# The attention mixer of a small transformer tower, rewritten for fp32 heads in strips of TensorE

## The reference, cut to what matters

```python
E, H, D = 192, 12, 16
h = _ln(x, ln1_g, ln1_b)                     # x is _layernorm(h), a second norm follows at once
qkv = h @ in_w.T + in_b
q, k, v = (t.reshape(B, N, H, D) for t in jnp.split(qkv, 3, axis=-1))
scores = jnp.einsum('bqhd,bkhd->bhqk', q, k) / jnp.sqrt(jnp.float32(D))
attn = jax.nn.softmax(scores, axis=-1)
ctx = jnp.einsum('bhqk,bkhd->bqhd', attn, v).reshape(B, N, E)
x = x + ctx @ out_w.T + out_b
x = x + gelu(x @ mlp_w1 + mlp_b1) @ mlp_w2 + mlp_b2
# ... then a gated mixture of 4 experts, whose output is added
```

## Time and profile before

| | us |
|---|---|
| three runs | 1097.98, 1101.22, 1106.42; median 1101.22 |
| the profiled execution | 1104.34 |
| its span, first to last instruction | 1102.6 |
| mixer, first instruction to the first of experts | 463.8 to 761.5, 297.7 |
| busy over the whole span | PE 897.6, DVE 610.5, ACT 526.0, POOL 228.3 |

### The profile page before, as it was taken

How to read it: one execution, slowest core, us unless ns; L and a number is a source line. 1 busy time by engine, 2 the same in 40 slices (tenths; PEclk the granted TensorE clock), 3 DMA queues, 4 the chain that set the end, 5 groups by cost and what they waited for, 6 DMA issues and landing times. The chain is left out here.

```text
span 1102.6 us, 18700 instructions
## 1 busy us (share of the span) xinstructions
PE 897.6 (81%) x5796; PEld 779.1 (71%) x5796; DVE 610.5 (55%) x1588; ACT 526.0 (48%) x1432; POOL 228.3 (21%) x303
## 2 busy tenths in 40 slices
PE   0069999999999999538568688784689999999997
PEld 0058989889898988526447476572568879889786
DVE  5834244342434333168978868684435765756754
ACT  2335353544445344126426557383346555465564
POOL 6202020110202021056730000000015223241250
PEclk9999999999999999955556766777779999999999
DMA  7152233242423323233210000002010010010000
GB/s 207 68 129 69 63 74 78 60 105 55 109 59 76 78 57 101 74 99 101 63 50 18 7 21 4 11 4 71 0 34 1 1 48 0 0 48 0 15 1 15
DMA packets 48901, 57.18 MB, mean 52 GB/s; under 512 B 7456, under 2 KB 43936, under 8 KB 48864
## 3 DMA queue, kind: packets, MB, share of 16 engines
q1 hardware_dynamic: 41568, 44.20, 15.3%
q0 software_dynamic: 2368, 8.46, 2.6%
q10 hardware_dynamic: 4928, 4.07, 1.7%
HBM read 37.83 MB, written 18.87 MB: 51 GB/s over the span
## 5 line engine op out<-in xcount | busy, mean ns | idle before, releaser
L1526 DVE TENSOR_TENSOR ffn_hid_lo<-ffn_gelu,ffn_hid_hi 128x512 fp32r<-128x512 f32 x120 | 95.9, 802 | 116.0 <-ACT ffn_hid_hi L1504 106.3
L1465 PE MATMUL ffn_ps_out<-ffn_weights_w,ffn_hid_hi 128*128 128x384 f32 x480 | 146.5, 362 | 3.1 <-DVE ffn_hid_lo L1526 1.9
L1501 ACT ACTIVATE ffn_gelu<-ffn_ring,ffn_b 128x512 f32<-128x512 f32 x120 | 82.1, 684 | 125.8 <-PE ffn_ring L1454 122.9
L490 POOL TENSOR_SCALAR attn_probs<-attn_probs,attn_inverse 128x128 f32<-128x128 f32 x128 | 47.8, 373 | 358.5 <-DVE attn_inverse L713 350.7
L1466 PE MATMUL ffn_ps_out<-ffn_weights_w,ffn_hid_lo 128*128 128x192 f32 x480 | 121.3, 253 | 0.0
L1465 PEld LDWEIGHTS ffn_ps_out<-ffn_weights_w,ffn_hid_hi 128*128 128x128 f32 x480 | 90.2, 188 | 13.7 <-DVE ffn_total L1584 4.1
L1466 PEld LDWEIGHTS ffn_ps_out<-ffn_weights_w,ffn_hid_lo 128*128 128x128 f32 x480 | 91.5, 191 | 4.3
L637 ACT ACTIVATE attn_probs<-ps_scores,attn_neg_max 128x128 f32<-128x128 f32 x128 | 45.2, 365 | 82.2 <-DVE attn_neg_max L709 82.2
L1017 ACT ACTIVATE mix_probs<-mix_ps_scores,mix_neg_max 128x128 f32<-128x128 f32 x192 | 67.5, 376 | 29.9 <-DVE mix_inverse L1102 17.0
L1504 ACT ACTIVATE ffn_hid_hi<-ffn_gelu 128x512 fp32r<-128x512 f32 x120 | 75.9, 632 | 3.8
L720 DVE COPY attn_mixed_rows<-ps_pairs 128x256 f32<-128x256 f32 x32 | 13.6, 425 | 88.3 <-PE ps_pairs L572 50.9
(11 more groups left out here) (299 smaller groups left out, 2661.6 us busy)
## 6 DMA issues: line engine op xcount, KB each, us to landing
v_rows<-attn_v_flat SPq DMA_DIRECT2D x16, 768.0 KB, 3.2
attn_v_rows<-v_rows SPq DMA_DIRECT2D x128, 96.0 KB, 3.3
mix_stage<-in_w POOLq DMA_DIRECT2D x5, 576.0 KB, 5.7
embed_stage_main<-in_w_qkv SPq DMA_DIRECT2D x3, 768.0 KB, 5.6
mix_raw_in<-in_w POOLq DMA_DIRECT2D x10, 192.0 KB, 3.1
mix_raw_in<-in_w POOLq DMA_DIRECT2D x5, 384.0 KB, 4.1
attn_xin<-h_rows ACTq DMA_DIRECT2D x8, 192.0 KB, 4.5
last_emb<-h_rows SPq DMA_DIRECT2D x8, 192.0 KB, 2.5
```

The source lines that it names most:

```text
L490: last = nc.gpsimd.tensor_scalar(probs[:, n, j, :], probs[:, n, j, :], inverse[:, n, j:j + 1], float(D) ** -0.5, ALU.mult, ALU.mult)
L1465: nc.tensor.matmul(ps_out[:, b, 0:2 * D], hid_hi[:, i % 3, tile], w2[:, c, :, :], start=c == 0, stop=False)
L1501: nc.scalar.activation(gelu[:, i % 2, :], ring[:, bank(slot), :], ACT.Gelu, bias=b1[:, f * HC + c:f * HC + c + 1]).then_inc(chunk_read.sem, 1)
L1526: nc.vector.tensor_tensor(hid_lo[:, i % 3, :], gelu[:, i % 2, :], raw(hid_hi[:, i % 3, :]), ALU.subtract).then_inc(lo_ready.sem, 1)
```

## The change

`mixer` is rewritten, in straight-line code without a loop: a list `order` gives the steps for all 16 tiles.

- q and k are no longer doubled into hi and lo. A strip of 32 rows holds two heads of 16 features; for the first eight heads the scores of one strip are one fp32 matmul of 256 columns, in which k is once masked to the even and once to the odd head. The other four heads (`tail`) are one matmul of 128 columns in each strip. Q and k need three projections of 128 output rows per unit, not six. 1/4, the scaling of the scores, goes into q.
- After the maxima (DVE, two instructions of 128x768), four fp32r matmuls of 384 columns with the identity add the negative maximum to the scores in PSUM (`lower`), and `exp` is two ACT instructions of 128x768 per tile, without bias and without sum.
- The transposes stay; the transposed probabilities are copied once, in fp32, by ACT only.
- P.V: v is stationary, padded to 32 columns per head (16 of them zero), and the transposed probabilities stream, 128 columns of one head at a time, in four column strips: 12 fp32 matmuls, whose result is the context already turned, features in the partitions. Four more matmuls of 384 columns with a block of ones give the sums on the same partitions. DVE takes the reciprocal of 128x384 sums and multiplies 128x384.
- Out: three fp32 matmuls of 192 columns, with a host-padded weight.
- The second norm takes its variance from the first (`spread_2`), so one pass over the rows serves both; the residual is formed in place in `hin`, which holds all 16 tiles.
- Outside `mixer`: POOL loads and splits the mixer's weights at the start of `attention`. Before its last turn SP waits for the stores of the turn before and reads 14 tiles of `h1` into `hin`; the last two follow at the start of `mixer`. The raw weights of the nets have buffers of their own, so that POOL starts on them at once.

The core of the diff:

```diff
@@ attention @@
+            for b in range(UNIT):
+                sp.wait_ge(h1_stored[b].sem, h1_stored[b].at(UNITS - 2, 0))
+            sp.dma_start(keep["hin"][:, 0:EARLY, :], dram["h1"][0:EARLY * P, :].rearrange("(b p) d -> p b d", p=P)).then_inc(keep["hin_loaded"], 16)
             body(UNITS - 1, False)
...
+            for part, (to, of) in enumerate(((slice(0, P), slice(0, MAIN)), (slice(0, TAIL), slice(MAIN, D)), (slice(TAIL, P), slice(MAIN, D)))):
+                pool.dma_start(mix_raw[to, min(part, 1), :], dram["w_mix"][of, :]).then_inc(mix_loaded, 16)
+            pool.wait_ge(mix_loaded, 48)
+            nc.gpsimd.tensor_scalar(mix_hi[:, :], mix_raw[:, 0, :], 1.0, 1.0, ALU.mult, ALU.mult)
+            nc.gpsimd.tensor_scalar(mix_half[:, :], mix_raw[:, 1, :], keep["low_rows"][:, 0:1], 1.0, ALU.mult, ALU.mult).then_inc(mix_hi_ready, 1)
...
+            nc.gpsimd.tensor_tensor(mix_lo[:, :], mix_raw[:, 0, :], raw(mix_hi[:, :]), ALU.subtract)
+            nc.gpsimd.tensor_tensor(mix_stack[:, :], mix_raw[:, 1, :], raw(mix_half[:, :]), ALU.subtract)
@@ mixer: the order of work @@
+        norms(0, range(NORM_PARTS))
+        projections(0, "X Q0 Q1 Q2 V0 V1 V2 V3")
+        for t in range(TILES + 1):
+            unit, j = divmod(t, UNIT)
+            if t < TILES:
+                order.append(("S", t))
+            if t:
+                order.append(("T", t - 1))
+            if t < TILES:
+                order.append(("M", t))
+            if t == 0:
+                norms(1, range(NORM_PARTS))
+            elif unit + 1 < UNITS and j == 0:
+                norms(unit + 1, range(10, NORM_PARTS))
+            if t:
+                order.append(("A", t - 1))
+            if unit + 1 < UNITS:
+                projections(unit + 1, {0: "", 1: "X Q0", 2: "Q1 Q2", 3: "V0 V1 V2 V3"}[j])
+            if unit + 2 < UNITS and j > 1:
+                norms(unit + 2, {2: range(0, 5), 3: range(5, 10)}[j])
+            if t:
+                order.append(("O", t - 1))
@@ mixer: TensorE @@
+            def scores(t):
...
+                if t:
+                    pe.wait_ge(exps_ready, 2 * t)
+                for i in range(STRIPS):
+                    rows = slice(32 * i, 32 * i + 32)
+                    nc.tensor.matmul(ps_scores[:, i, 0:2 * P], q_main[rows, unit % 2, tile_of(t)], k_main[rows, unit % 2, b, :, :].rearrange("p a k -> p (a k)"), start=True, stop=True)
+                for i in range(STRIPS):
+                    rows = slice(32 * i, 32 * i + 32)
+                    last = nc.tensor.matmul(ps_scores[:, i, 2 * P:WIDE], q_tail[rows, unit % 2, tile_of(t)], k_tail[rows, unit % 2, b, :], start=False, stop=True, skip_group_check=True)
+                    if i % 2:
+                        last.then_inc(scored, 1)
+            def lower(t):
...
+                for h in range(2):
+                    pe.wait_ge(max_ready, 2 * t + h + 1)
+                    for i in (2 * h, 2 * h + 1):
+                        wide = neg_max[:, i, :].unsqueeze(2).to_broadcast([P, SETS, P])
+                        last = nc.tensor.matmul(ps_scores[:, i, 0:WIDE].rearrange("p (s k) -> p s k", k=P), ident_r[:, :], wide, start=False, stop=True, skip_group_check=True)
+                    last.then_inc(lowered, 1)
+            def mix(t):
...
+                for s in range(SETS):
+                    for i in range(STRIPS):
+                        rows = slice(32 * i, 32 * i + 32)
+                        nc.tensor.matmul(ring[rows, bank("A", t, 0), s * P:(s + 1) * P], v_pad[:, unit % 2, b, i * SETS + s, :], pt[:, i, s, :], start=True, stop=True)
+                slot_free("A", t, 1)
+                for i in range(STRIPS):
+                    rows = slice(32 * i, 32 * i + 32)
+                    last = nc.tensor.matmul(ring[rows, bank("A", t, 1), 0:WIDE], ones[:, :], pt[:, i, :, :].rearrange("p s k -> p (s k)"), start=True, stop=True)
+                last.then_inc(mixed, 1)
+            def project_out(t):
+                pe.wait_ge(context_ready, t + 1)
...
+                for s in range(SETS):
+                    last = nc.tensor.matmul(ring[:, bank("O", t), 0:D], context[:, s, :], w_out[:, s, :], start=s == 0, stop=s == SETS - 1)
@@ mixer: ScalarE @@
+            def exps(t):
+                for h in range(2):
+                    act.wait_ge(lowered, 2 * t + h + 1)
+                    nc.scalar.activation(probs[:, halves(h), :, :].rearrange("p i s k -> p i (s k)"), ps_scores[:, halves(h), 0:WIDE], ACT.Exp).then_inc(exps_ready, 1)
+            def turned_probs(t):
+                for i in range(STRIPS):
+                    act.wait_ge(turned, STRIPS * t + i + 1)
+                    nc.scalar.activation(pt[:, i, :, :], ring[:, bank("T", t, i), 0:WIDE].rearrange("p (s k) -> p s k", k=P), ACT.Copy).then_inc(pt_ready, 1)
@@ mixer: VectorE @@
+            def normalise(t):
+                by_set = lambda part: ring[:, bank("A", t, part), 0:WIDE].rearrange("p (s k) -> p s k", k=P)
...
+                steps.then(nc.vector.reciprocal(inverse[:, :, :], by_set(1)))
...
+                nc.vector.tensor_tensor(context[:, :, :], by_set(0), inverse[:, :, :], ALU.mult).then_inc(context_ready, 1)
```

More of the change, by code:

```diff
@@ L817, in mixer @@
[L817 to L823 removed]
+        NORM_PARTS = 15
@@ new lines, in mixer, with norms, projections @@
+        order = []
+        def norms(unit, parts):
+            order.extend(("N", (unit, part)) for part in parts)
+        def projections(unit, steps):
+            order.extend(("X", unit) if s == "X" else (s[0], (unit, int(s[1:]))) for s in steps.split())
+        norms(0, range(NORM_PARTS))
[20 more added lines that the diff above has]
+                order.append(("O", t - 1))
@@ L970, in project_qk @@
                 if s == 0:
-                    pe.wait_ge(weights_ready, 1)
-                slot_free(turn, slot, source)
+                    pe.wait_ge(zt_ready, 2 * unit + 2)
                 cols = slice(s * P, (s + 1) * P)
                 passes = ((w_hi, zt_hi, 0), (w_hi, zt_lo, 0), (w_lo, zt_hi, 0), (w_stack, zt_hi, 1), (w_stack, zt_lo, 1))
-                for i, (w, z, part) in enumerate(passes):
-                    last = nc.tensor.matmul(ring[:, bank(slot), :], w[:, cols], z[:, part, :], start=i == 0, stop=i == 4)
@@ L977, in project_qk, with project_v @@
-                last.then_inc(ring_filled.sem, 1)
-            def project_v(turn, b, slot, hi, source):
-                slot_free(turn, slot)
+                for k, (w, z, part) in enumerate(passes):
+                    last = nc.tensor.matmul(ring[:, bank("Q", i), :], w[:, cols], z[:, part, :], start=k == 0, stop=k == 4)
+                last.then_inc(q_filled, 1)
+            def project_v(i):
+                unit, b = i
+                slot_free("V", i)
                 tile = slice(b * P, (b + 1) * P)
```

536 lines of the change are left out of this document (234 added, 302 removed).

## The result

| | median us | lowest to highest | ratio to the kernel before, 95% interval |
|---|---|---|---|
| before | 1102.93 | 1097.98 to 1106.42 | |
| changed | 1072.24 | 1068.92 to 1073.63 | 0.9721 (0.9674 to 0.9767) |
| changed, measured again beside two of the experiments | 1073.60 | 1072.61 to 1076.32 | 0.9731 (0.9694 to 0.9768) |

The forecast was 1071, 30 us less than before; the change gave 31. The profiled execution has a span of 1071.9 us. The windows of the changed mixer, from its first instruction to the first of `experts`: way in, three units, and the last unit with its tail. They answer to the earlier trace rows. The columns are those of the earlier trace rows; the seventh figure is the granted clock.

What follows compares the result with a forecast made beforehand. Steps waiting for each other and a clock of 0.69 bound the mixer, no engine being full. Its terms summed to 264.5 against 297.7 us; less 3 in attention, 30 gained: 1071, range 1022 to 1108 (own range 1055 to 1090).

Steps and rivals of the forecast that it cites:

- The mechanism: In every tile the out projection waits for DVE's context, and the next scores queue behind it; 9.3 us at full clock.
- The reciprocal: DVE's reciprocal of 128x384 sums in each tile, priced at 2.3 us by the slope of two small rows.
- The two dear cases: Rival: DVE's reciprocal takes 3.2 us (kernel 1085) or 5.1 us (kernel 1116) in each tile; chance 0.15.
- a similar clock: TensorE in the mixer: load about 80% at clock 0.69, like before, so the middle, 56 us for a full unit.
- the forecast's own two prices of each stretch: Mixer units at full clock and 1.2 GHz: full unit 49 and 63 us, third 43 and 61, last 58 and 69.
- The way in: Mixer's start before its first unit: 29.5 us against 36.2, with 3 us waiting for constants on DVE.
- The first unit: Mixer's first four tiles: 69 us against 85.3; tile 0 at 23 with 7.6 of stalls, the others 46.
- Attention: Loss before the mixer: 2 us from POOL's work on the first norm, 1 from the early read of `h1`; 3 together.
- The cold case: Rival: TensorE never gets full clock, as its pauses are longer than before; 1100 us, chance 0.05.
- the strips' case: Rival: fp32 strips overlap only in part, two deep, in scores and P.V with sums; 1125 us, chance 0.13.
- the cheap reciprocal's price: Rival: reciprocal at 0.55 us, each tile's wait 1.75 shorter, 28 us over 16 tiles; chance 0.22 shared with a warm clock.
- My rival: Cheap reciprocal or a warm clock in the mixer: 1043 us, with full clock throughout 1020; chance 0.22.

Runs made afterwards that it cites:

- filler run: Changed kernel with useless fp32 matmuls given to TensorE in its pauses before out projections and the next unit's first projection; 1066.11 us, ratio 0.9674.
- residual run: Changed kernel with the first unit's residual formed on DVE behind the split of z instead of before it; 1072.81 us, ratio 0.9726.
- the run shows 48: Changed kernel with the reciprocal of the sums replaced by a copy of the same 128x384 elements; 1024.05 us, ratio 0.9296.
- strip run: Changed kernel with the twelve P.V matmuls issued strip by strip instead of going round the four strips; 1081.10 us, ratio 0.9803.

## Why the prediction was right, and where it wasn't

**The mechanism held.** TensorE's out projection waits for `mix_context`, and the next scores stand behind it, though in ten tiles and not in every one: in the others projections stand in front of it, which wait for DVE themselves (10.6 us in all for the split of z, 5.1 for a bank). The tile at full clock was forecast at 9.3 us and is 9.33, and with the reciprocal replaced 7.32. That it agrees to 0.03 is luck in part: the reciprocal in it is 0.26 longer than forecast, and the rest that much shorter. The scores are 0.86 us (0.86 forecast), P.V 0.68 and the sums 0.75 (0.72 and 0.67), the copies of the probabilities 0.49, the exps 0.83 (0.8), the product 0.56 (0.54). All were priced from starts of other shapes in the trace of before, and fp32 strips do overlap four deep when neighbours in the queue are on different strips.

**The reciprocal** was 2.3 by the slope of the earlier trace rows and is 2.56: 6.25 ns per element where the two small rows gave 5.5. Two rows 0.011 us apart can't give a slope much better; 16 x 0.26 is 4 us. The two dear cases, 3.2 and 5.1 us, are out. The reading of the page named in the prediction ("VectorE: DVE Perf Modes" of the Trainium skill, section "First, the fixed hardware budget"), eight cycles an element, gave 3.2 as an estimate; the measured slope is six cycles of the 0.96 GHz that the page states, and the measurement decides.

**The clock** was the step that failed: "a similar clock" of 0.69, since the load on TensorE would be alike, and so the middle between the price at full clock and at 1.2 GHz. The granted clock is 0.83 to 0.86 behind the first unit, so about 30% of the time is at 1.2 GHz and not half. With that share the forecast's own two prices of each stretch give, as an estimate, 54, 48 and 55 us for the second, third and last unit; 54.4, 49.3 and 53.2 were measured, 56, 52 and 58 forecast. Most of the 1.6, 2.7 and 4.8 us that were too much is this. Why the clock is higher isn't shown. TensorE stands idle longer in a middle unit than before (busy for 38.9 of 54.4 us against 52.4 of 65.2), and yet it was granted 0.83 and not 0.69, so to be alike in load was no ground for a forecast. The filler run shows one part: filling the pause brings 0.81 to 1.00 in the last unit. Left unfilled, the same pause of 3.27 us is followed by an out projection and scores at full clock in one tile (684.95 and 686.12), by both at 1.2 GHz in the next (694.27), and by an out projection at full clock and slow scores in the one after (706.26 and 707.43).

**The way in** is 34.1, not 29.5. The constants kept the norm waiting for the 3 us that were forecast (467.06 to 470.19). But I had laid "DVE forms the residual before it splits z" at the 2.2 us that it takes alone, and had counted POOL's stalls only for tile 0. The L1110 step beside POOL takes 7.21 us instead of 1.25 (as in the residual run's rows); these 5.96 are more than the 4.6 that were missing, so something else in the term was priced too high. The earlier trace rows showed the effect on one step, 2.54; the way in had no term for it, and a group of four steps in series lasts until the last of POOL's instructions ends (489.42 and 489.31). Moving DVE's work away showed that this isn't 6 us to be had: POOL has to be moved.

**The first unit**, 71.8 against 69, is in part the same cause: 22.4 for the first tile (23 forecast, with 7.6 of stalls; right), but 49.4 for the other three instead of 46, with 5.5 of stalled norm steps in the third tile where 4 had been put down. The granted clock of these three tiles is 0.71, much as forecast; the other 2 us aren't attributed.

**Attention** cost 3.3 (3 forecast). TensorE's first instruction came 2.7 to 3.3 us later (67.22 and 67.80 against 64.49), and 0.6 to 2 us of that went away in the three runs in which POOL's split of the mixer's weights was held back behind the first norm (66.62, 65.78, 65.99). The early read of `h1` cost nothing that shows: the last rows of v are awaited for 0.95 us, as in the earlier trace rows.

**The rivals.** The cold case and the strips' case are out by the rows above. Of the cheap reciprocal's price, 28 us, the run shows 48: a stall of 6 us missed by chance, and in the last unit the clock's loss, which goes with the pause. My rival had a cheap reciprocal and a full clock as separate steps, 1043 and 1020; where TensorE sets the pace they come together. No run takes single parts of the rewrite back towards the kernel before, so how the 31 us are shared among them is only priced, not shown. It also stays open how the clock's loss is to be reckoned ahead of time. It follows pauses of about 3 us in some tiles and not in others with the same work (9.33 and 11.09 us stand side by side).

## What to carry to other kernels

Price a chain by the instruction that stands in it alone, not by busy shares: here 2.6 us of DVE, in every tile that has no norm steps, set the pace of a kernel in which no engine was full, and giving TensorE the next scores to do in that time gave 19 to 20 us without making anything cheaper. Where one engine's work holds up another's, moving the work that is held up gained nothing, as it met the next of the same instructions (one run here); move the other, and place it by the time at which it runs, not by its place in a third engine's stream. And a forecast whose sum is right while its terms are off by 5 us with both signs is luck in part: check the terms.

## What the runs showed of the hardware that wasn't expected

- A reciprocal on DVE is 0.16 us and 6.25 ns per element of a partition, from 144 to 384 elements in PSUM, and within 0.015 us of that for the four and six of the earlier trace rows; a copy of 384 is 0.56.
- Beside POOL's instructions on SBUF, DVE's steps from SBUF to SBUF wait for whole instructions of POOL (four scalings 1.24 to 7.20 us, a step of four elements 0.16 to 2.53), while maxima, reciprocals and products, which read PSUM, and the statistics of a norm (1.13) don't. The page "SBUF — State Buffer" of the Trainium skill (section "Who interferes with whom") says that a DVE instruction with two SBUF inputs contends with one of GpSimd that reads SBUF, that one in a mode that takes both ports contends with GpSimd too, and that then the loser blocks fully; the rows agree in that DVE waits for whole instructions, and show it for steps of four elements.
- An exchange of ACT's table is 1.28 us, and in the tile shown it started 0.4 us before the instruction that needed it could, when ACT's exps were done, so little of it was hidden.
- Matmuls on one column strip don't keep later ones on other strips from starting; in the strip run records of the sums start between those of P.V that are ahead of them in the program.
